# Two of four row blocks turned by transposing DMA instead of by TensorE, in three of four batches of a gated cross-attention and mixture-of-experts kernel

## What is computed

```python
sim = einsum('bhnd,bhmd->bnm', Q, K) / (sqrt(d) * H)
mask = sim >= kth_largest(sim, int(0.3 * n))
A = sigmoid(sim) * mask;  A = (A + A.T) / 2
x = x + tanh(g_xattn) * ((1 - gamma) * layernorm(x) + gamma * A)
xn = layernorm(x)
shared = (silu(xn @ Wg.T) * (xn @ Wy.T)) @ Wd.T
top2, w = top_k(sigmoid(xn @ gate_w.T) + gate_bias, 2)
x = x + tanh(g_ffn) * (shared + sum over the two experts of w * expert(xn))
```

## Time and profile before

| | us |
|---|---|
| median of 3 runs (lowest, highest) | 539.08 (538.72, 540.26) |
| the profiled execution | 540.25 |
| its span on the core | 538.4 |
| PE busy | 488.7 (91%) |
| DVE busy | 328.4 (61%) |
| ACT busy | 254.3 (47%) |
| POOL busy | 219.9 (41%) |
| SP's queue of DMAs (q1), share of 16 engines' span | 25.0% |

### The profile page before, as it was taken

How to read it: one execution, slowest core, us unless ns; L and a number is a source line. 1 busy time by engine, 2 the same in 40 slices (tenths; PEclk the granted TensorE clock), 3 DMA queues, 4 the chain that set the end, 5 groups by cost and what they waited for, 6 DMA issues and landing times.

```text
span 538.4 us, 10344 instructions
## 1 busy us (share of the span) xinstructions
PE 488.7 (91%) x2992; PEld 266.9 (50%) x2993; DVE 328.4 (61%) x721; ACT 254.3 (47%) x465; POOL 219.9 (41%) x229
## 2 busy tenths in 40 slices
PE   7467988999898997999899999999999999999991
PEld 2234433544344443454446666666656656565650
DVE  2999897899868995689976773333323332323330
ACT  3874696889388946531315562222222222222220
POOL 2023367606773396302331443334443334444322
PEclk9758798999999998999999999999999999999997
DMA  5430333354435441330076986655665655566533
GB/s 197 153 103 2 120 103 84 84 179 141 124 83 174 147 110 35 138 103 2 0 271 196 244 213 115 121 101 97 107 102 105 114 108 97 99 110 106 105 40 39
DMA packets 45477, 61.57 MB, mean 114 GB/s; under 512 B 20544, under 2 KB 20800, under 8 KB 45440
## 3 DMA queue, kind: packets, MB, share of 16 engines
q1 hardware_dynamic: 36272, 40.53, 25.0%
q0 software_dynamic: 8736, 20.45, 22.0%
q10 hardware_dynamic: 432, 0.13, 0.1%
HBM read 37.90 MB, written 19.14 MB: 106 GB/s over the span
## 4 chain that ended last, share of the span: by engine, by line
PE 47%; DVE 32%; issue 8%; ACT 5%; DMA 3%; POOL 2%; DVEq 0%; ACTq 0%; POOLq 0%
PE py L1140 13%; PE pg L1120 12%; PE pu L1121 12%; DVE w L1238 5%; DMA out<-rows,idx 3%; PE pa L1130 2%; DVE work L1406 2%; PE pt_bank L896 2%; DVE pa L1268 2%; DVE w L1295 2%; DVE w L1285 2%; DVE w L1217 2%; DVE w L1603 1%; DVE w L1272 1%; ACT w L675 1%
## 5 line engine op out<-in xcount | busy, mean ns | idle before, releaser
L1120 PE MATMUL pg<-w,x_t 128*128 x408 | 123.3, 313 | 0.2
L1121 PE MATMUL pu<-w,x_t 128*128 x408 | 123.3, 313 | 0.0
L578 POOL DMA_INDIRECT out<-rows,idx x39 | 61.8, 1585 | 139.4 <-ACT rows L829 116.8
L962 PE MATMUL pg<-w 128*128 128x512 f16 x288 | 81.5, 402 | 6.0 <-DVE work L1406 6.0
L1140 PE MATMUL py<-w,work 128*128 x351 | 82.1, 379 | 0.8 <-DVE work L1666 0.8
L819 ACT ACTIVATE work<-pg 128x352 f32<-128x352 f32 x39 | 18.0, 463 | 125.5 <-PE pu L1121 125.3
L514 POOL TENSOR_TENSOR w<-stage,w 128x544 f16<-128x544 f32 x42 | 54.2, 1301 | 37.3 <-ACT stage L624 30.2
L962 PE MATMUL pu<-w 128*128 128x512 f16 x240 | 66.7, 388 | 0.0
L620 ACT ACTIVATE w<-stage 128x544 f16<-128x544 f32 x80 | 50.9, 648 | 26.9 <-DMA stage<-in_weights 26.3
L1666 DVE COPY work<-pa 128x768 f16<-128x768 f16 x39 | 21.8, 558 | 61.2 <-PE pa L1130 61.1
L1655 DVE SCALAR_TENSOR_TENSOR work<-pu,work 128x352 f32<-128x352 f32 x39 | 20.5, 525 | 62.7 <-ACT work L819 62.6
(11 more groups left out here) (245 smaller groups left out, 781.7 us busy)
## 6 DMA issues: line engine op xcount, KB each, us to landing
stage<-in_weights SPq DMA_DIRECT2D x80, 272.0 KB, 3.1
xn_rows<-w SPq DMA_DIRECT2D x16, 256.0 KB, 2.8
out<-w SPq DMA_DIRECT2D x16, 256.0 KB, 2.4
w<-in_x SPq DMA_DIRECT2D x3, 1024.0 KB, 5.3
w<-in_ctx_t SPq DMA_DIRECT2D x4, 256.0 KB, 3.9
w<-in_x SPq DMA_DIRECT2D x2, 512.0 KB, 3.7
out<-rows,idx POOLq DMA_INDIRECT x39, 4.9
work<-xn_rows,idx POOLq DMA_INDIRECT x20, 4.5
```

The costliest lines, as they stand in the source:

```text
L578: pool.indirect_dma_start(out=out, out_offset=bass.IndirectOffsetOnAxis(ap=idx[:, t:t + 1], axis=0), in_=rows[:, t % 2, :], in_offset=None ...
L962: mm = pe.matmul(bank_[:, :], w[:, half, part, at:at + P], x_tb[:, xpart * KC + k, :], start=(k, part, xpart) == (0, 0, 0), stop=(k, part) ...
L1120: pe.matmul(pg[p][:, 0:H], lhs, w[:, item, half, at:at + H], start=begin, stop=end)
L1121: mm = pe.matmul(pu[p][:, 0:H], lhs, w[:, item, half, at + H:at + 2 * H], start=begin, stop=end)
```

## The change

For batches 1 to 3, SP issues a transposing transfer of row blocks 0 and 1 from `xnr` straight into `x_tb`, each ahead of that block's store. It waits for the block's low and high parts and for the shared expert's last read of `x_tb` (`up_mm`). A new semaphore `xt_ld` counts the landings. PE's turns of these blocks, DVE's copy of block 0 and ACT's copy of block 1 are gone. `logits(b)` waits for both landings ahead of its first product; the writers that reuse `xnr` (ACT's `normalised`, DVE's `check`) wait for them too. Batch 0 stays as it was. `turned(b)` and `copied(b)` count PE's turns and each engine's copies anew; all other edits carry these counts.

```diff
+        xt_ld = sem("xt_ld")
...
-        ROWS_DVE = BATCHES * (TPB // 2)
+        def turned(b):
+            return TPB + (b - 1) * (TPB // 2) if b else 0
+
+        def copied(b):
+            return turned(b) // 2
+
+        def by_transfer(b):
+            return b * (TPB // 2) * 16 - TPB // 2 * 16 if b else 0
+
+        ROWS_DVE = copied(BATCHES)
...
                 for i in range(b * TPB, (b + 1) * TPB):
                     after(sp, xn_lo, i + 1)
                     after(sp, xn_hi, i + 1)
+                    if b and i % TPB < TPB // 2:
+                        after(sp, up_mm, b * UPS)
+                        sp.dma_start_transpose(out=x_tb[:, :, i % TPB * P:(i % TPB + 1) * P], in_=xnr[:, i % TPB, :]).then_inc(xt_ld, 16)
                     sp.dma_start(xn_tiles[:, i:i + 1, :], xnr[:, i % TPB:i % TPB + 1, :]).then_inc(xn_st, 16)
...
                 if i == 0:
                     after(act, xn_st, b * TPB * 16)
-                    after(act, xt_mm, b * TPB)
+                    after(act, xt_mm, turned(b))
+                    after(act, xt_ld, by_transfer(b))
...
             def rows_turned(b, i):
-                if i == 1:
-                    after(act, up_mm, b * UPS)
-                after(act, xt_mm, b * TPB + i + 1)
+                after(act, up_mm, b * UPS)
+                after(act, xt_mm, turned(b + 1) - TPB + i + 1)
                 act.activation(x_tb[:, :, i * P:(i + 1) * P], xt_banks[i % 2], ACT.Copy).then_inc(xt_act, 1)
...
                 for i in range(1, TPB):
                     normalised(b, i)
-                rows_turned(b, 1)
...
             def turn_batch(b, i):
-                if i == 0:
+                if i == (TPB // 2 if b else 0):
                     after(pe, lg_sb, b)
                     after(pe, hid_sb, b * UPS)
-                    after(pe, xt_act, b * (TPB // 2))
+                    after(pe, xt_act, copied(b))
                 after(pe, xn_hi, b * TPB + i + 1)
                 after(pe, xn_lo, b * TPB + i + 1)
                 if i == 2:
-                    after(pe, xt_sb, b * (TPB // 2) + 1)
+                    after(pe, xt_sb, copied(b) + (b == 0))
                 if i == 3:
-                    after(pe, xt_act, b * (TPB // 2) + 1)
+                    after(pe, xt_act, copied(b) + (b == 0))
...
             def logits(b):
-                after(pe, xt_sb, (b + 1) * (TPB // 2))
+                after(pe, xt_ld, by_transfer(b + 1))
+                after(pe, xt_sb, copied(b + 1))
                 for i in range(TPB):
                     if i == TPB - 1:
-                        after(pe, xt_act, (b + 1) * (TPB // 2))
+                        after(pe, xt_act, copied(b + 1))
...
                     shared_down(b, 1)
-                    turn_batch(b + 1, 0)
-                    turn_batch(b + 1, 1)
                     shared_down(b, 2)
                     turn_batch(b + 1, 2)
                     turn_batch(b + 1, 3)
...
                     shared_down(b, 2)
-                    turn_batch(b + 1, 0)
-                    turn_batch(b + 1, 1)
                     shared_down(b, 3, range(0, 3))
...
                 after(dve, xn_st, b * TPB * 16)
-                after(dve, xt_mm, b * TPB)
+                after(dve, xt_mm, turned(b))
+                after(dve, xt_ld, by_transfer(b))
...
                         score_stats(b + 1, (i,))
-                    after(dve, up_mm, b * UPS)
-                    rows_turned(b, 0)
                     shared_rows(shared, 1)
...
                     low_rows(3, None)
-                    after(dve, up_mm, b * UPS)
-                    rows_turned(b, 0)
                     shared_rows(shared, 2)
```

More of the change, by code:

```diff
@@ L595, in _ @@
                 if t + GATHERS < SLOT_TILES:
-                    after(pool, xt_mm, TILES + t + 1)
+                    after(pool, xt_mm, turned(BATCHES) + t + 1)
                     if t >= BY_DMA:
@@ L792, in router_exp @@
                 act.activation(r[1][:], r[0][:], ACT.Exp, scale=-UP_UNSCALE).then_inc(exp_ok, 1)
-            after(act, xt_act, BATCHES * (TPB // 2))
+            after(act, xt_act, copied(BATCHES))
             act.activation(warm[:], warm[:], ACT.Exp)
@@ L811, in _ @@
             after(act, xn_st, TILES * 16)
-            after(act, xt_mm, TILES)
+            after(act, xt_mm, turned(BATCHES))
             after(act, up_mm, BATCHES * UPS)
@@ L1396, in rows_turned @@
             def rows_turned(b, i):
-                after(dve, xt_mm, b * TPB + i + 1)
+                after(dve, up_mm, b * UPS)
+                after(dve, xt_mm, turned(b + 1) - TPB + i + 1)
                 dve.tensor_copy(x_tb[:, :, i * P:(i + 1) * P], xt_banks[i % 2]).then_inc(xt_sb, 1)
@@ L1668, in gathered_turned @@
             def gathered_turned(t, p, uses, bank_=xt_ps, blocks=2 * KC):
-                after(dve, xt_mm, TILES + t + 1)
+                after(dve, xt_mm, turned(BATCHES) + t + 1)
                 after(dve, up_mm, Q0 + uses)
```

## The result

The changed kernel takes 544.69 us (median of 4 runs, 543.06 to 545.73) against 539.29 for the kernel before in the same comparison (4 runs, 538.72 to 540.26): ratio 1.0095, 95% interval 1.0075 to 1.0115. It is slower by 5.1 us (by the ratio; the medians lie 5.4 apart); 8.3 were forecast.

The account below looks back on a forecast made before the run. DVE's way round, 58.1 us a batch, was taken as the bound. Losses of 3.8 + 3.8 + 0.7 us in the three seams gave +8.3: 548.6 from the profiled 540.25, 547.4 for the median; range 539.0 to 551.0.

Parts of the forecast that it names:

- The mechanism: First two seams: PE's router products wait for the second landing, delaying DVE's chain by 3.8 us each.
- rival 1: Seams: no fall of PE's clock; 2.1 us lost in each of the first two, 0.7 in the third; 544.0, chance 0.14.
- The issue: SP's queue: issuing a 128 by 1024 transfer takes 2.06 us, bounded by 1.19 and 2.38.
- rival 2: SP's queue: the issue doesn't grow from 1.19 us; sum about 0, 539.1 us, chance 0.12.
- The part after the issue: DMA: from the issue's end to the landing 1.84 us, with ends of 1.2 and 7.0.
- rival 4: All seams: slow landing, 4.1 us after the issue, each seam losing 2.3 more; +15.2, 554.3 us, chance 0.11.
- signs of being wrong: Changed profile: issues near 1.2 us, a landing under 3 us after the first start, or an unchanged period despite PE's standstill.
- the clock's price: PE behind the standstills of the first two seams: a clock fall costing 1.67 us each, with ends of zero and 1.67.
- The cover: Load of x behind the transfers: costs nothing because DVE is itself 3.8 us late; without that, 0.5 a seam.
- Removed work: Turns and copies taken out: DVE gains 0.15 us a seam, limited by POOL's spread; PE gains 0.7 in the third seam.
- The rule: Skill's statement that transposing transfers are as fast as regular ones, 350 to 400 GB/s; rows showed 129 and 192.
- The third rival: Seams: a transfer is as cheap as a store, saved copies count fully; 538.1 or 537.0 us, chance 0.09.

Follow-up runs that it names:

- early: The changed kernel with both transfers of a seam issued between the two `store_shared`: 537.61 us, ratio 0.9969 to the kernel before.
- late: The changed kernel with both transfers of a seam issued behind the four row stores: 552.08 us, ratio 1.0233 to the kernel before.
- split: The changed kernel with each transfer cut into two of 128 by 512 values: 552.79 us, ratio 1.0260 to the kernel before.
- only1: The changed kernel with transfers in the first seam alone, the other batches as before: 542.43 us, ratio 1.0045 to the kernel before.
- filled: The changed kernel with eight unread PE matmuls ahead of the landing wait in the first two seams: 542.89 us, ratio 1.0047 to the kernel before.
- beside: The kernel before plus the six transfers into an idle buffer nobody reads, PE still turning all blocks: 540.49 us, ratio 1.002.
- early3: As early, with block 2 by transfer too, three a seam: 537.99 us, ratio 0.9959 to the kernel before.

## Why the prediction was right, and where it wasn't

**The mechanism was right.** (The range is wide, from 539.0 to 551.0, and rival 1's 544.0 lies in it as well; what supports the mechanism are the waits and the experiments, not the time.) The first two seams lose because PE's products wait for the second landing and DVE's `shared_hidden` in turn for PE: the waits of 2.03 and 3.63 us, the 14 us between `early` and `late`, and the equal times of `early` and of the kernel without transfers show it. Where PE's clock fell, it cost 1.7 us in the second seam, as forecast (1.67).

**The issue was the mis-sized term.** The step "so I let that part stay and the other 0.87 double: 2.06 us" gave 2.06; the trace has 1.27, near the lower bound of 1.19. The reason given against rival 2, that "something in it counts blocks", fell too: `split` shows that two halves cost two issues. With 1.27 in place of 2.06 the second landing of a seam is 1.6 us earlier, so the working gives 1.3 + 1.67 - 0.8 = 2.2 for each of the first two seams (measured alone: 2.4 and 3.3), a landing ahead of PE in the third, so -0.7 there (measured -1.0, with no change in its interval), and 3.7 in all. The measured 5.1 lies between this and the 8.3.

**The part after the issue was right in five landings of six.** 1.84 was forecast, and 3.1 less 1.27 = 1.8 is the median. The sixth decides the second seam: 4.8 less 1.26 = 3.5, 1.7 more than forecast, on the way to rival 4's 4.1. That puts the second seam at 2.2 + 1.7 = 3.9 and the sum at 5.4. This is worked out afterwards, and why that landing was slow stays open.

**Its own signs.** Of the prediction's signs of being wrong one came true, issues near 1.2 us. The standstills were 2.03, 3.63 and none, where 3.8, 3.8 and 1.5 had been forecast; the clock fell behind one of the first two in this profile, not behind both; and the period of 58.1 us grown to about 62 was 58.9 from the first seam to the second (171.54 less 112.68). Measured alone, the seams gave 2.4, 3.3 and -1.0, where 3.8, 3.8 and 0.7 had been forecast: each term was too large.

**Rival 1 is the nearest by its number, and that is luck.** It gave 544.0, and 544.69 was measured. But its condition, that the clock doesn't fall, is not met (0.51 in the second seam, 0.52 in the first seam alone, and 2.6 us less with the standstills filled), and it used the issue of 2.06. Two mistakes cancelled: too long an issue, and no price for the clock.

**Why rival 2 didn't come true with it.** It had the right issue and gave a sum of about 0, since it left out the clock and the slow landing of the second seam. The prediction tied the clock's price to the longest standstill; the profiles show it behind shorter ones too, 2.40 us in `only1` and 1.89 in `split`, and not behind the 2.03 of the changed kernel. `filled`, which changes little else, took away about half of the loss. That such a standstill may or may not be followed by a fall was not foreseen; the prediction asked of it a yes or a no.

**The cover was weaker than claimed.** The load of x was costed at nothing because DVE would be late itself. `beside` puts its price at 1.1 us for all seams (0.5 a seam had been worked out without the cover), and the changed kernel's statistics wait for it by 0.40. The store ahead of the load was taken to land as before; here it took 4.84 us.

**Removed work.** DVE's 0.15 a seam by POOL's row was right (0.1 measured in the first). In the third seam PE's gain was 1.3 less the 0.2 brought along, 1.1, not 0.7.

**The rule and the rows.** The third rival fell: it needed the second landing 2.9 us after the first transfer's start, and a transfer's issue took 1.27 us against a store's 0.32, with none of the six landing in under 3.0. The data moved at some 210 GB/s where the stores moved at 370 to 447 (last section). The Trainium skill (Advanced Engine Details and Errata, X-Bar Transpose (TRN2)) has such transfers as fast as regular ones; at this size the trace disagrees.

## What to carry to other kernels

Before moving work from an engine to a DMA, find the place in the issuing queue and compute the landing from there; the data's readiness says little when the queue waits for something else. Here the same six transfers lost 5 us behind one `store_shared` and gained 1.7 in front of it. Take the issue time from a measured transfer of the same kind before scaling it with its size: here half the size cost as much, and this was the largest error. Count a standstill of PE at the granted clock's price too, as a chance rather than a yes or a no. Keep a load's wait on the chain even where the forecast happens to cover it, since a better forecast of another term uncovers it. And look at the granted clock ahead of the changed stretch before comparing two profiles: 0.68 us of this pair's difference arose before the change had done anything.

## What the runs showed of the hardware

The issue of a transposing transfer took 1.25 to 1.34 us for 128 by 1024 values in the changed kernel (up to 1.71 in `early3`), and 1.19 for 128 by 512: it hardly depends on the columns, and two halves cost twice (2.5 to 2.6). The DMA engines moved the second transfer of the first seam at about half of the stores' rate; the DMA view of the stretch from 115.2 to 118.5 us, GB/s in 40 slices, has the transfer in the seventeenth to thirtieth number and the stores behind it from there on:

```profile
GB/s 9 62 279 289 295 279 289 445 422 447 397 323 273 298 298 280 214 177 217 223 230 205 202 217 202 220 195 223 195 186 308 379 422 372 397 447 397 372 397 373
```

About 210 GB/s against 370 to 447. The Trainium skill, DMA: Bandwidth & Descriptors, Latency and other measured facts, has 261 GB/s for a transposing DMA with a non-contiguous middle dimension, which this destination has; this trace is below it.

The granted clock fell to 1.2 GHz (0.50 to 0.52) behind standstills of PE of 1.89, 2.40, 3.63 and 4.37 us (`split` in its third seam, `only1`, the changed kernel, `split` in its first), and stayed at full behind the changed kernel's 2.03 and behind a longer one ahead of all transfers:

```profile
81.55 0.81 PE L975 MATMUL pg<-w 128*128 128x512 f16 x3 [2.69 <-DVE work L1413]
```

So the length of the standstill alone didn't decide it here. What does isn't shown.
